# A two-block kernel on one core: in layer two's expert tiles, the next group's turns move ahead of the former group's down products, and the gated rows' turns go last

## What is computed

```python
xn = _layernorm(x)
s = _L0_attn_ref(xn, ...)                 # causal softmax attention, 16 heads of 16
g = _silu(_L0_ffn_ref(xn, ...))           # 16 experts, top 4, width 256
x = x + s * g
xn = _layernorm(x)
s = _L1_attn_ref(xn, ...)                 # linear attention with elu, silu gates, layernorm
g = _silu(_L1_ffn_ref(xn, ...))           # 32 experts, top 4, width 96, and a shared expert of 512
x = x + s * g
```

```python
g = jnp.einsum('th,ehi->eti', x, w_gate)
u = jnp.einsum('th,ehi->eti', x, w_up)
hmid = jax.nn.silu(g) * u
routed = jnp.einsum('eti,te,eih->th', hmid, combine, w_down)
```

## Time and profile before

| | |
|---|---|
| median of the runs | 428.37 us (427.02 to 430.78, three runs) |
| span of the profiled execution | 462.5 us |
| PE busy with matmuls | 421.1 us (91% of the span) |
| PE loading weights (overlaps) | 327.6 us (71%) |
| DVE busy | 329.8 us (71%) |
| ACT busy | 234.4 us (51%) |
| POOL busy | 216.2 us (47%) |

### The profile page before, as it was taken

One profiled execution on the slowest core, in us unless ns is written; L12 is line 12 of the kernel. 1 busy time (PEld: TensorE's weight loads), 2 busy tenths in 40 slices (PEclk: granted clock), 3 DMA queues, 4 the chain that ended last, 5 costly groups with the idle time before them and its releaser, 6 DMA issues.

```text
span 462.5 us, 10086 instructions
## 1 busy us (share of the span) xinstructions
PE 421.1 (91%) x3213; PEld 327.6 (71%) x3213; DVE 329.8 (71%) x1135; ACT 234.4 (51%) x596; POOL 216.2 (47%) x208
## 2 busy tenths in 40 slices
PE   8899999899999998998989899958988999969696
PEld 4757899798999997656666684646766774645585
DVE  5886699978866667588999988525576664344685
ACT  3373233434433436878899636315566568124421
POOL 2023688767643320778880101655576602747400
PEclk9999999999999999589999999979999999979889
DMA  8937888888999982379776760233555523323202
GB/s 246 409 142 240 319 275 268 250 258 279 282 312 308 316 277 69 79 195 211 150 172 187 268 210 7 85 87 114 166 145 149 165 92 116 107 63 104 68 23 68
DMA packets 42274, 84.17 MB, mean 182 GB/s; under 512 B 7136, under 2 KB 27104, under 8 KB 41584
## 3 DMA queue, kind: packets, MB, share of 16 engines
q1 hardware_dynamic: 30656, 60.99, 39.6%
q0 software_dynamic: 9936, 20.85, 18.5%
q10 hardware_dynamic: 1632, 1.71, 1.1%
HBM read 65.81 MB, written 15.60 MB: 176 GB/s over the span
## 4 chain that ended last, share of the span: by engine, by line
PE 63%; DVE 14%; issue 8%; ACT 6%; another core or an unknown queue 4%; DMA 3%; SPq 1%; POOL 1%; ACTq 0%; DVEq 0%
PE ps L1169 14%; PE ps L1120 7%; PE ps L1185 7%; PE ps L1147 4%; PE ps L1289 4%; PE ps L964 3%; PE ps L1264 3%; PE ps L1106 3%; PE ps L1377 3%; ACT til L835 2%; PE ps L948 2%; PE ps L967 2%; DMA experts<-in_gu 2%; PE ps L1158 2%
## 5 line engine op out<-in xcount | busy, mean ns | idle before, releaser
L544 POOL DMA_INDIRECT til<-xn_rows,gidx x71 | 71.0, 999 | 98.1 <-PE ps L1158 43.4
L1169 PEld LDWEIGHTS ps<-til,experts 128*128 128x128 f32 x752 | 90.6, 192 | 8.1 <-issue 3.9
L1169 PE MATMUL ps<-til,experts 128*128 128x128 f32 x752 | 92.1, 276 | 3.2 <-DVE til L1645 1.5
L708 ACT ACTIVATE til<-ps 128x256 f32<-128x256 f32 x47 | 18.0, 382 | 66.2 <-PE ps L1158 66.2
L835 ACT ACTIVATE til<-til,mxs 128x128 f32<-128x128 f32 (+1 forms) x128 | 49.0, 453 | 0.0
L1185 PE MATMUL ps<-experts,til 128*128 x188 | 48.4, 381 | 0.0
L1120 PE MATMUL ps<-experts,til 128*64 x192 | 36.1, 345 | 9.4 <-issue 9.4
L756 ACT ACTIVATE til<-ps,wtile 128x256 f32<-128x256 f32 x95 | 42.0, 471 | 2.5 <-PE ps L1149 2.4
L1769 DVE CUSTOM_DVE_ANT_0 til<-ps,cst 128x128 f32<-128x128 f32 (+1 forms) x128 | 37.8, 352 | 5.7 <-PE ps L1264 3.3
L1120 PEld LDWEIGHTS ps<-experts,til 128*64 128x64 f32 x192 | 26.7, 144 | 15.5 <-issue 12.2
L1122 PE MATMUL ps<-xn,til 128*64 128x192 f32 x192 | 36.2, 345 | 0.0
(11 more groups left out here) (240 smaller groups left out, 959.4 us busy)
## 6 DMA issues: line engine op xcount, KB each, us to landing
experts<-in_gu SPq DMA_DIRECT2D x47, 512.0 KB
sorted_rows<-til SPq DMA_DIRECT2D x95, 128.0 KB
experts<-in_gu SPq DMA_DIRECT2D x8, 768.0 KB
experts<-in_dn SPq DMA_DIRECT2D x4, 1024.0 KB, 11.0
experts<-in_dn SPq DMA_DIRECT2D x8, 384.0 KB
experts<-att SPq DMA_DIRECT2D x44, 32.0 KB
til<-xn_rows,gidx POOLq DMA_INDIRECT x71
xr<-in_x SPq DMA_DIRECT2D x2, 512.0 KB, 4.2
```

Of the source, the lines that this page charges most:

```text
L544: po.indirect_dma_start(to, None, xn_dram[s.n], bass.IndirectOffsetOnAxis(ap=gidx[:, t:t + 1], axis=0))\
L1169: mm = pe.matmul(ps[:, b0, m * P:(m + 1) * P], gw[:, j, k * w + m * P:k * w + (m + 1) * P], xgT[:, j % 2, k, :], start=(k == 0), stop=(k = ...
```

## The change

It reorders the steps of layer two's tile loop on three engines. On PE the list is replaced by a loop that does, for each g: up products of g, turns of g + 1, down products of g - 1, the experts' numbers of g + 1, turned rows of g. The turns of group 0 come ahead of the loop, the down products of group 11 behind it. ACT's and DVE's lists are reordered to suit: ACT does the gates of g, then the copy of the turns of g + 1; both kinds of copies of second down weights (for group g - 1) come ahead of the gates; DVE adds the biases ahead of its gate products. No instruction is added or removed, and POOL's and SP's programs stay as they are. The first hunk lets a stage have a negative lag.

```diff
             for g in range(NT1 // 4 + max(lag for lag, _ in stages)):
                 for lag, work in stages:
-                    if 0 <= g - lag < NT1 // 4:
+                    if max(0, -lag) <= g - lag < NT1 // 4:
                         work(g - lag)
@@ ACT
-                    run_double_tiles([(0, turn_four), (1, copy_second), (2, weigh_second), (0, gate_four), (2, silu_rows), (1, weigh_first), (0, copy_first)])
+                    turn_four(0)
+                    run_double_tiles([(2, weigh_second), (1, copy_first), (1, copy_second), (2, silu_rows), (0, gate_four), (-1, turn_four), (1, weigh_first)])
@@ PE
-                    run_double_tiles([(0, experts_of_four), (0, turn_four), (1, turn_h_four), (0, up_four), (1, down_four)])
+                    groups = NT1 // 4
+                    experts_of_four(0)
+                    turn_four(0)
+                    for g in range(groups):
+                        up_four(g)
+                        if g + 1 < groups:
+                            turn_four(g + 1)
+                        if g >= 1:
+                            down_four(g - 1)
+                        if g + 1 < groups:
+                            experts_of_four(g + 1)
+                        turn_h_four(g)
+                    down_four(groups - 1)
@@ DVE
-                    run_double_tiles([(0, first_copies), (1, turned_four), (0, gate_four), (0, copy_four), (1, biases), (3, products)])
+                    run_double_tiles([(0, first_copies), (1, turned_four), (1, copy_four), (1, biases), (0, gate_four), (3, products)])
```

## The result

The change makes the kernel slower by a little: 431.55 us median (429.65 to 434.88, 15 runs) against 428.44 (425.84 to 432.33, 15 runs), a ratio of 1.0077 with a 95% interval of 1.0059 to 1.0096. That is 3.3 us, between 2.5 and 4.1, and so within the 1% bound. The forecast was 430.5, or +2.1. (One of ten runs of `before_again` took 687.31 us and one of nine of `delay_old` 1047.8; they are slow runs, which the ratios leave out.)

A forecast was written before the change was run, and what follows sets the result against it. PE was taken to bound the kernel before and after, with the profiled stalls likelier than not absent from timed runs: 428.37 + 1.6 (joints) + 0.5 (end) = 430.5 us, range 423.0 to 433.0.

The forecast's parts named there:

- What bounds the kernel: Layer two's tile stage: PE sets the pace, 5.99 us a group; the profiled 8.2 us of late copies likelier absent when timed.
- The gap: PE's wait ahead of up products goes, ACT's copy gets 2 us of slack: -8.2 us if stalls are timed, else 0.
- The joints: PE's switches between full-width and half-width work, four a group instead of two: +0.15 us a group, +1.6 us taken.
- The 0.04 us wait for the copy: Old order, turned rows to up products: some 0.04 of the 0.25 us is PE waiting for ACT's copy.
- ACT and DVE at nothing: Reordered lists on ACT and DVE cost 0, with cover of 2 us on ACT and 1.3 on DVE.
- POOL and SP at nothing: Same programs and DMAs; a gather burst of 5.73 us has two periods, 12.3, to land: cost 0.
- The end: Group 11's down products start 1.64 us behind the last turned rows, waiting for DVE's copies, instead of 1.10: +0.5 us.
- C: Rival: gathers pace the new order by holding PE's signals, 6.45 us a group, +4.5 us, 432.9; chance 0.14.
- D: Rival: nothing measurable; timed old-order stalls of 0.1 to 0.4 us a group pay for the joints, 426.5 to 429; chance 0.14.
- A span of 456 to 459: The changed kernel's profiled span in us, from the profiled 462.5 - 8.2 + 1.6 + 0.5 = 456.4.
- PE bound before and after: The main case: PE sets the pace in both orders, 430.5 us, 428.9 to 431.4 by the joints' bounds; chance 0.50.

The follow-up runs named there:

- before_again: The kernel before with no edit, profiled and timed once more: 428.05 us, ratio 1.0002.
- delay_old: The kernel before with two more ACT copies of 128x384 per group (1.07 us) between the gates and what follows: 430.98 us, ratio 1.0047.
- delay3_old: The kernel before with three more ACT copies of 128x384 per group (1.6 us) between gates and copy of the turns: 437.38 us, ratio 1.0196.
- delay3_new: The kernel after with three more ACT copies of 128x384 per group (1.6 us) between gates and copy of the turns: 433.23 us, ratio 1.0101.
- act_only: The kernel before with only ACT's list as changed, PE and DVE as before: 426.54 us in one run.
- tail_copies_first: The kernel after with DVE's copies of down weights ahead of its copies of the turned rows: 432.6 us, ratio 1.0119.
- delay_new: The kernel after with two more ACT copies of 128x384 per group (1.07 us) ahead of the copy of the turns: 431.05 us, ratio 1.0053.
- more_joints: The kernel after with its turned rows split in two, one part between the two pairs of down products: 434.69 us, ratio 1.0172.

## Why the prediction was right, and where not

- **What bounds the kernel.** Right: PE in both, with 5.99 us a group in the old order. The prediction got that from one group beside no gathers and from the 34 us between profile and median. The reason it gave, that PE's signals are held "only (or mostly) while the profiler records", doesn't hold: the profiles of `before_again` and of the kernel after were taken by the same profiler, have gathers beside their groups, and show no such wait. Recording alone doesn't make it, and why one execution had it is open.
- **The gap.** Right for the case taken (0 us), and `delay3_old` and `delay3_new` show that the mechanism works as described where there is a gap: 2 us of slack for the copy were claimed, and 1.6 are hidden.
- **The joints.** Right mechanism, term too small: +0.15 a group between the starts was forecast and is there, but a group grew by 0.24. The step measured only the distance across a joint. The matmul behind it is late too, by 0.04 to 0.05. +1.6 became +2.4, which is within the bound of 2.5; that bound came from another cause (0.25 as the true price of a joint), so that it holds is luck. The rule of the Trainium skill ("TensorEngine Tiling (Array Packing)", section "Tiling Modes") that a change of mode drains TensorE agrees with the sign; the size is the trace's.
- **The 0.04 us wait for the copy** in turned rows to up. It is there, as put, and `act_only` shows that it's the transposes that the copy waits for.
- **ACT and DVE at nothing.** Right: no idle PE in 50 us.
- **POOL and SP at nothing.** Wrong, by 1.0 us in the profiled execution. That a burst has two periods to land holds for full groups. For group 2 the bursts start only with the stage, and its turns were moved ahead of 1.8 us of down products that had hidden the rest of the landing. All executions show the spread: from the first turn to group 2's up products, the old order takes 16.9 to 17.1 us in four of them, the new one 17.3 to 18.5 in six (0.24 of it joints). Two of the six, the kernel after and `tail_copies_first`, lose 1.0 and 1.3 by the start. `delay_new`, `delay3_new` and, with its joints taken off, `more_joints` lose about 0.1 or less. So the term is real, but 1.0 isn't its usual size as far as the traces show.
- **The end.** 1.64 forecast, 1.68 measured; +0.5 forecast, +0.58 measured. Two small errors cancel in the 1.64: the two copies of turned rows hold DVE for 0.67, not 0.75, and the handing over takes 0.27, not 0.15.
- **Rivals.** C falls: gathers pace no full group, and six traces have 6.23 or, with more joints, 6.51 in every group from group 3 on. Where gathers do hold PE is the start. D, the old order paying 0.1 to 0.4 us a group for late copies, falls too: it pays 0.04 and has 0.66 of slack in ACT.
- **A span of 456 to 459** was wrong: it took the exceptional execution for the profile of every kernel. The sum made against the median was the one to keep.

By its terms: 428.4 + 2.4 + 1.0 + 0.6 is 432.4, against 431.55 measured; 0.9 of the traces' 4.0 us isn't in the medians' difference of 3.1, and the interval, up to 4.1, holds it only just. With 0.1 for the start, as in `delay_new`, the sum is 431.5. That the start of most timed runs is of that kind would explain the 0.9, but isn't shown, since only profiled executions show their start.

The forecast of +2.1 is two thirds of the 3.1. Its own range for PE bound before and after, 428.9 to 431.4, was missed by 0.15 us: the path was right, one term was a third too small and another left out.

No order tried here beats the kernel before. `act_only` equals it by its trace.

## What to carry to other kernels

Before a reordering that takes a stall away, ask whether the stall is in the runs that are timed: if the profiled span and the median are far apart, profile again, or trust the stretch that runs as fast as the median needs. Count joints between full-width and half-width work on PE as a cost, with the matmul behind them, since an engine that is busy throughout pays for each. And price a moved step in the first and last rounds of its loop too: here 0.7 of 3.1 us (`delay_new`) to 1.6 of 4.0 (the kernel after) came from there.

## What the hardware showed that was not expected

- A switch of PE between 128x128 work and two column halves costs 0.09 to 0.10 us at the joint and another 0.04 to 0.05 at the next matmul; two more of them in each group took 0.28 us, once as 0.24 (5.99 to 6.23) beside a wait of 0.04 that went, once in full (6.23 to 6.51).
- In one execution of the kernel before, ACT's second gate started 348.30 - 346.75 = 1.55 us behind the end of PE's last up product while gathers ran; in the same kernel profiled again it is 302.59 - 302.55 = 0.04. That PE's signal is what came late is argued, since the profile can't name the releaser. That execution's view of waits for the stretch 300 to 382 us has the line below (us in total, times, longest). In the eleven other traces, of the same kernel and its variants, no wait of this stage has an unnamed releaser.

```profile
ACT til L727 <- remote: 14.9, 7, 2.6
```

- Three small ACT copies in each group make the same gap as that execution. A stall's shape in the timeline doesn't tell its cause.
